# The layer norm of the second pair of sequences, moved within the opening pair's round from the attention units of layer 1 to the end of that layer

## The reference

```python
# layer 0
mu = jnp.mean(x, axis=-1, keepdims=True)
var = jnp.mean(jnp.square(x - mu), axis=-1, keepdims=True)
h = (x - mu) * jax.lax.rsqrt(var + LN_EPS)
h = h * (1.0 + scale[:, None, :]) + shift[:, None, :]
q = h @ Wq.T; c_kv = h @ Wkd.T; k = c_kv @ Wku.T; v = c_kv @ Wvu.T
...
x = x + out
# layer 1
attn = jax.nn.softmax(scores, axis=-1)
ctx = jnp.einsum('bkgst,bktd->bkgsd', attn, v)
x = res + ctx @ Wo.T
h = ada_rms(x, time_emb, ln2_w, ln2_tw)
mlp = jax.nn.silu(h @ Wg.T) * (h @ Wu.T) @ Wd.T
return x + mlp
```

## Time and profile before

| what | value |
|---|---|
| runs, median of 3 | 1804.85 us (1804.28 to 1805.57) |
| profiled execution, span from first to last instruction | 1804.9 us |
| mean granted clock of TensorE | 0.974 |
| TensorE busy | 1717.2 us, 95% |
| VectorE busy | 1152.3 us, 64% |
| ScalarE busy | 945.9 us, 52% |
| GpSimd busy | 398.8 us, 22% |
| chain that ended last | TensorE 77%, VectorE 10%, transfers 6% |

### The profile page before, as it was taken

The page is one execution under the profiler, slowest core; times in us unless marked ns, Lnnn a source line. Parts: engine busy times, 40 slices in busy tenths (PEclk is TensorE's granted clock), DMA queues, the critical chain, the costliest instruction groups (busy, mean ns, idle before and its releaser), DMA issues.

```text
span 1804.9 us, 37773 instructions
## 1 busy us (share of the span) xinstructions
PE 1717.2 (95%) x12440; PEld 931.9 (52%) x12440; DVE 1152.3 (64%) x2858; ACT 945.9 (52%) x2769; POOL 398.8 (22%) x556
## 2 busy tenths in 40 slices
PE   6686899999999999999999999999999999999999
PEld 2344445555455545555455554555455554555444
DVE  6759566675667657685576756676576855767320
ACT  3836456364664538564483646645385644835320
POOL 3438587011111112111110111111121111101120
PEclk9676999999999999999999999999999999999999
DMA  7866489462784449662593637944485725936220
GB/s 245 152 181 115 126 197 253 98 117 82 163 175 94 80 119 184 133 118 78 127 194 91 119 88 161 171 95 82 115 192 125 123 73 138 196 85 112 100 70 24
DMA packets 527231, 234.30 MB, mean 130 GB/s; under 512 B 476336, under 2 KB 493744, under 8 KB 527024
## 3 DMA queue, kind: packets, MB, share of 16 engines
q1 hardware_dynamic: 511472, 175.09, 48.9%
q10 hardware_dynamic: 15552, 56.63, 10.1%
HBM read 90.09 MB, written 16.78 MB: 59 GB/s over the span
## 4 chain that ended last, share of the span: by engine, by line
PE 77%; DVE 10%; DMA 6%; issue 4%; ACT 2%; SPq 1%; DVEq 0%; POOL 0%; ACTq 0%
PE up L1427 8%; PE up L1429 8%; PE up L1428 8%; PE gate L1427 7%; PE gate L1429 7%; PE gate L1428 7%; PE y L1427 4%; PE y L1428 4%; PE y L1429 4%; PE bank L1427 4%; PE bank L1429 4%; PE bank L1428 4%; DMA prob_t<-prob 3%; PE bank L1454 2%; DVE prob L1113 2%
## 5 line engine op out<-in xcount | busy, mean ns | idle before, releaser
L864 ACT ACTIVATE bank<-bank,low 128x128 f32<-128x128 f32 (+2 forms) x768 | 302.7, 395 | 68.2 <-DVE low L1106 35.0
L702 POOL TENSOR_TENSOR inner_t<-inner,inner_t 128x512 f16<-128x512 f32 x128 | 149.0, 1164 | 662.7 <-ACT inner_t L1045 662.6
L1113 DVE TENSOR_TENSOR prob<-bank,prob 128x512 f16<-128x512 f32 (+1 forms) x320 | 202.8, 634 | 54.3 <-ACT prob L873 53.4
L873 ACT ACTIVATE prob<-bank 128x512 f16<-128x512 f32 (+1 forms) x320 | 178.7, 558 | 73.3 <-DMA prob_t<-prob 44.5
L1427 PE MATMUL up<-mlp,ring 128*128 128x512 f16 x512 | 194.9, 381 | 12.8 <-DVE inner L1392 12.8
L1382 DVE SCALAR_TENSOR_TENSOR silu<-silu,gate 128x512 f32<-128x512 f32 x128 | 87.9, 687 | 183.8 <-ACT silu L1039 183.0
L1427 PE MATMUL gate<-mlp,ring 128*128 128x512 f16 x512 | 194.0, 379 | 1.4 <-DVE mlp L1078 0.9
L1429 PE MATMUL up<-mlp,ring 128*128 128x512 f16 x512 | 194.9, 381 | 0.0
L1428 PE MATMUL up<-mlp,ring 128*128 128x512 f16 x512 | 194.9, 381 | 0.0
L1429 PE MATMUL gate<-mlp,ring 128*128 128x512 f16 x512 | 194.0, 379 | 0.0
L1428 PE MATMUL gate<-mlp,ring 128*128 128x512 f16 x512 | 193.9, 379 | 0.0
(11 more groups left out here) (182 smaller groups left out, 4041.8 us busy)
## 6 DMA issues: line engine op xcount, KB each, us to landing
ring<-wgu_dram ACTq DMA_DIRECT2D x108, 512.0 KB, 3.8
x_in<-x_dram SPq DMA_DIRECT2D x18, 512.0 KB, 3.8
x_res<-x_mid SPq DMA_DIRECT2D x16, 512.0 KB, 3.0
wgu_dram<-ring SPq DMA_DIRECT2D x16, 512.0 KB, 3.6
out_dram<-x_res SPq DMA_DIRECT2D x32, 256.0 KB, 2.3
prob_t<-prob SPq DMA_TRANSPOSE x256, 3.5
inner_t<-wd_t_dram SPq DMA_DIRECT2D x4, 1024.0 KB, 8.7
ring<-wg_t_dram SPq DMA_DIRECT2D x16, 256.0 KB, 4.1
```

The source lines that it names most:

```text
L702: pool.tensor_tensor(inner_t[:, 1, f, :], inner[:], inner_t[:, 0, f, :], ALU.subtract).then_inc(inner_low, 1)
L864: ins = act.activation(bank_[:, at:at + wid], bank_[:, at:at + wid], ACT.Exp, bias=low[:, j % BANKS, k:k + 1], scale=-1.0, accum_out=total)
L873: act.activation(terms(prob[:, g % SLOTS, 0, :], layer, j), terms(work_bank[USE[f"unit{layer}", j] % BANKS][:], layer, j), ACT.Copy).then_ ...
L1113: dve.tensor_tensor(terms(prob[:, slot, 1, :], layer, j), terms(work_bank[USE[name] % BANKS][:], layer, j), terms(prob[:, slot, 0, :], lay ...
```

## The change

In the opening round alone, VectorE's `units` no longer calls `ln_stats` and `ln_apply`. They are called in `finish` of layer 1: the statistics of a sequence right behind its tile 1 weighting, the subtraction right behind its tile 1 head remainder. On GpSimd the roots of the layer norm move, in that round, to the step `fill4.0`, ahead of the roots of the RMS norm. All other rounds are as before. The change was described in a few words as one by which GpSimd's norm roots come ahead of the rope angles; in the other rounds they stand ahead of them before and now, and in the opening round the program has them behind, as the rows on GpSimd below show.

```diff
--- before.py
+++ after.py
@@ -714,11 +714,15 @@
                             for f in range(EARLY):
                                 chunk_scale(f)
                                 chunk_halves(f)
+                    if m is None:
+                        if step == "fill4.0":
+                            for s in BOTH:
+                                ln_root((n[0], n[1] + 1), s)
+                    elif step in LN_STATS:
+                        ln_root((n[0], n[1] + 1), LN_STATS[step])
                     if step in ("fill2.0", "fill4.0"):
                         for s in BOTH:
                             root(n, ("fill2.0", "fill4.0").index(step), s)
-                    if step in LN_STATS:
-                        ln_root((n[0], n[1] + 1), LN_STATS[step])
                     if step == ANGLES_AT:
                         need_apart(pool, full, count(n, USES, USE["unit0", UNITS[0] - 1] + 1),
                                    (half_made, 1))
@@ -1140,7 +1144,9 @@
                 for j in range(total):
                     step = f"unit{layer}_{j}"
                     between(m, step)
-                    if step in LN_STATS:
+                    if m is None:
+                        pass
+                    elif step in LN_STATS:
                         ln_stats((n[0], n[1] + 1), LN_STATS[step])
                     elif step in LN_APPLY:
                         ln_apply((n[0], n[1] + 1), LN_APPLY[step])
@@ -1278,11 +1284,16 @@
                 between(m, f"out{layer}a.0", f"out{layer}a.1")
                 for s in BOTH:
                     add(n, layer, s, 0)
+                late = m is None and layer == 1
                 for s in BOTH:
                     normalise(n, layer, s, 1)
+                    if late:
+                        ln_stats((n[0], n[1] + 1), s)
                 between(m, f"heads{layer}.0", f"heads{layer}.1")
                 for s in BOTH:
                     heads_low(n, layer, s, 1)
+                    if late:
+                        ln_apply((n[0], n[1] + 1), s)
                 between(m, f"out{layer}b.0", f"out{layer}b.1")
                 for s in BOTH:
                     add(n, layer, s, 1)
```

## The result

| | before | changed |
|---|---|---|
| median of 20 runs each | 1804.22 us (1801.41 to 1805.59) | 1807.46 us (1803.41 to 1812.66) |
| ratio | | 1.0021, interval 1.0014 to 1.0028 |
| profiled execution, span | 1804.9 us | 1802.2 us |
| its own time | not given | 1804.13 us |

The changed kernel is **slower by 3.2 us**, 0.2%, and its executions lie further apart. The forecast was no change, 1804.8, in a range of 1802.2 to 1807.4, and the median lies at its upper edge. The profiled executions mislead if they are compared by their spans: that of the changed kernel is one of its fastest, 3.3 us under its median, and that of before, if its own time too stands 1.9 us above its span, is slower than all 20 runs of its kernel.

The account below looks back on a forecast made before the run. It took VectorE to bound the opening's units, ScalarE next, and TensorE nearly all the rest. Units -4.15, statistics +2.1 and clock +2.0 sum to -0.05: no change, 1804.8 us, range 1802.2 to 1807.4.

Parts of the forecast that it names:

- Units stage, -4.15: Opening units 2 to 10: without layer norm on VectorE, ScalarE's 1.54 us pace sets 12.32 instead of 16.47 us, saving 4.15.
- End of layer 1, +2.1: Before the tile 1 projections: 2.84 us of statistics ahead of the head remainder, less hidden slack, delay TensorE by 2.1 us.
- Subtractions free, at 0.94 a pair: End of layer 1: subtractions behind the head remainders cost nothing, covered by the projection, at 0.94 us a pair.
- GpSimd free: Moved roots on GpSimd cost nothing: angles end at 177.1 us and the roots find it idle by 3.9 us.
- The clock, +2.0: Tile 1 projections: TensorE's longer hole before them makes its clock fall, costing 2.0 us, bounds 0 and 3.1.
- rival 2: Units stage: transfers, not ScalarE, set the pace, so the gain is only 2.45 us; 1806.5 us, chance 0.12.
- Rival 1: End of layer 1: TensorE's clock holds through the longer hole; sum -2.05, 1802.8 us, chance 0.18.
- rival 4: GpSimd: roots come behind the angles and delay subtraction and head remainder; +1.8 on the sum, 1806.6 us, chance 0.04.
- rival 3: Clock stays low from the last values through both pairs of projections; sum +4.0, 1808.9 us, chance 0.08.
- rival 5: ScalarE's pace to the last unit, clock holding, half the fall at 251 us saved; -3.6, 1801.2 us, chance 0.07.

Follow-up runs that it names:

- e8: The changed kernel run again, unedited, on another chip: 1807.11 us against 1804.20 for the kernel before, ratio 1.0017.
- e1: The changed kernel with statistics and subtractions moved behind both head remainders: 1804.89 us against 1805.32 for the kernel before, ratio 1.0004.
- e2: The changed kernel with 13 useless matmuls around the transposes in TensorE's hole: 1805.42 us against 1805.32 for the kernel before, ratio 1.0004.
- e5: The changed kernel with statistics and subtractions behind both head remainders, plus seven filler matmuls: 1811.55 us against 1804.20 for the kernel before.
- e12: The changed kernel with a fourth slot for `prob` in the opening round's layer 1: 1806.58 us against 1804.83 for the kernel before, ratio 1.0012.
- e6: The changed kernel with layer norm behind both head remainders, seven filler matmuls and a fourth `prob` slot: 1808.77 us against 1804.20 for the kernel before.
- e4: The kernel before with only the four subtractions moved behind the head remainders, statistics left among the units: 1805.26 us against 1805.32, ratio 1.0000.
- e3: The kernel before with the opening round's layer norm cut to 16 of 512 columns, in its old place: 1803.92 us against 1805.32, ratio 0.9993.
- e11: The kernel before with a fourth slot for `prob` in the opening round's layer 1: 1804.46 us against 1804.83, ratio 0.9997.
- e9: The kernel before with only the subtractions moved behind the head remainders, plus a fourth `prob` slot: 1804.29 us against 1804.83, ratio 0.9997.
- e10: The kernel before with seven useless filler matmuls in TensorE's hole: 1811.71 us against 1804.83, ratio 1.0035.

## Why the prediction was wrong

By its steps:

- **Units stage, -4.15: failed.** This is the step that made the forecast wrong. Measured on the path, in A: -1.4 (changed), -1.3 (e8), and -1.2 to -1.4 in e1, e2 and e5, under my lower bound of 2.45. The step took the transfers out of the sum because they "were late where VectorE had let units through in bunches". They were late in part for another reason, a transfer of instructions in front of them, and evenly paced units meet it too. The accounting of the changed kernel: 4.15 less 2.34 (nearly all of it the one late copy's wait of 2.12) is 1.81, plus 0.09 from units 10 to 15. Of these 1.90 another 0.5 never reaches TensorE: its first projection used to start 1.16 us ahead of the last remainder, now 0.66. There TensorE hangs behind, busy for 4.89 of 5.00 us in 170 to 175 against 3.83 before, at a clock of 0.50 until near 173 (windows above). The fourth slot confirms the first part: it takes 1.6 or 1.7 us off A in the changed kernel and off e5, and none off the kernel before. In e12 VectorE gains 4.16 us between units 2 and 10, the forecast's 4.15, but A is only 3.0 under the kernel before: the first projection, once 1.16 us ahead of the last remainder, now comes 0.12 behind it. What is missing lies at TensorE, which now waits 1.0 us for a transfer itself (e12's wait list, and 1.2 in e6's), and at its low clock.
- **End of layer 1, +2.1: right.** B grew by 2.08, and e1, by moving nothing but the place, brings it back to zero. (The 0.1 that the sum gives a semaphore is read from no row.)
- **Subtractions free, at 0.94 a pair: right** (0.99; B and C of e4 are those of before).
- **GpSimd free: right.** The roots found it idle by 7.50 us where 3.9 were forecast; the angles ended at 175.0, not 177.1, 1.4 of it since this execution began its units so much sooner.
- **The clock, +2.0: right in place and near in size.** C grew by 2.2 and 2.3. The medians give the fall 3.1, by e2; the interval around that is wider than the 0.9 between them.

With the measured terms the sum is -1.4 + 2.1 + 2.2 = +2.9, where the medians show +3.2. So the mechanism of **rival 2**, transfers as the pace of the units, with the forecast's clock was nearest; it priced the gain at 2.45 and the whole at 1806.5. Against it I had said "copies waited 1.7 us in all": true, but with the cover of the earlier trace rows over them, and I took the cover away in the same step. Rival 1 is refuted by the windows, rival 4 by GpSimd's timeline, rival 3 by the clock of 1.00 in 175 to 180. Part of rival 5, the fall saved near 251 us, happened in the first profiled execution alone, and was luck: e8 and every other profile have the fall.

By the Trainium skill (TensorE: Matmul & The Clock Gate, Part 4: PE-mode transpose) transposes don't count as TensorE being busy in the same way, and the forecast took from it that the fall would be certain. The fall came. But holes of the old length, with the same two groups of transposes, went both ways, as the windows of e4 and of e3 show, each 3.68 us ahead of the projections and then the projections. e4:

```profile
181.40:185.08 3.68, 1.96 (x28) 1.34 (x25) 3.00 (x7) 1.92 (x4) 2.97 (x6) 1.00 0.00 0
185.08:190.30 5.22, 5.22 (x24) 2.24 (x24) 2.96 (x6) 0.72 (x2) 0.82 (x2) 1.00 0.11 43
```

e3:

```profile
181.03:184.71 3.68, 1.80 (x27) 1.28 (x24) 2.87 (x7) 1.92 (x4) 2.13 (x5) 1.00 0.00 0
184.71:189.93 5.22, 5.22 (x17) 2.07 (x18) 1.38 (x2) 0.02 (x1) 0.00 (x0) 0.67 0.00 0
```

In e4 the clock held, in e3 it fell behind a hole that is the same to 0.2 us of work. In the kernel before and in e11 it held (1.97 and 1.96 us of work); in e1, e3 and e9, which start these projections sooner (1.79 or 1.80 us), it fell, and C is 1.6 or 1.7 us longer. The longest single wait in the hole was 0.7, 0.7 and 0.8 us where it held and 1.0 where it fell; six holes do not show that this is the cause. In e3 and e9 the fall is a second reason why the gain in the units did not come through, and one the forecast had not. In e1 it is not: there VectorE's queue sets the end.

**Open.** What decides, between holes so alike and between two executions of one program, whether the clock falls. What spreads E over 6 us between executions of one program, and with it how much of the clock's 3.1 us in the medians is real beyond 2.2. Whether shifted fetches make the 5 to 7 us that e5, e6 and e10 lose behind the opening, and why e2, with the same waits, shows no such loss. And the start of the units themselves lies between 147.3 and 149.6 us, on the average 0.9 sooner in the seven profiles with the layer norm's statistics late, though no instruction ahead of it differs; the table leaves that out.

## What to carry to other kernels

Before a term is taken off the bounding engine, list the waits that end under its cover (here 1.7 us of copies waiting for transfers, seen in the wait list) and charge them in full: a buffer's depth that costs nothing beside 2.5 us of other work costs 2 us without it. Work that is moved into a place where TensorE already idles costs its own length and may cost the clock too; where it must go there, it goes behind the instruction that TensorE waits for, and only as much of it as the cover holds: the subtractions alone were free there (e4), statistics, roots and subtractions together cost 2.3 us (e1). Before a cut-down kernel is taken for a bound, look how long the cut instructions still take: 16 columns in place of 512 left 2.11 us of 2.53 (e3). Compare stages between fixed instructions, with at least two profiles of the changed kernel: here the spans alone said that the slower kernel was 2.7 us faster.

## What was not expected of the hardware

- A transfer of instructions (16 KB, 1.67 us) holds up transposing packets that stand behind it, and with them the whole transposition: 4.6 us to landing at the median against 3.1, and a wait of 2.12 us of the copy that needs the slot. The Trainium skill (Advanced Engine Details and Errata, ISA Cache) gives 16 KB as the size in which instructions are cached, which agrees; what a fetch does to other transfers it doesn't say.
- Seven more TensorE instructions ahead of the long loop cost 6.9 us, nearly all behind them (e10), thirteen cost nothing that could be told (e2), though ScalarE's waits for transpositions in the loop nearly double in both (58.2 and 59.1 us against 30.8).
- Subtractions of 16 columns beside GpSimd's splits held VectorE for 0.80 and 2.11 us a pair, where those of 512 held it for 1.59 and 2.53 (e3).
- The same wait of 3.7 us brought the clock down in one execution and not in the next, a difference of 2.6 us in that place.
